# Perceiver on one core: a tile's eight row gathers issued together at its last step

## The reference

```python
x = x + _L0_ffn_ref(_layernorm(x, axis=-1), L0_ffn_gate_w, ...)         # 64 experts, 8 for each token
x = x + _L1_xattn_ref(_layernorm(x, axis=-1), ctx_1024, ctx_1024, ...)  # 8 heads, keys and values of both kinds
# _L0_ffn_ref, its end: each token's eight expert rows are weighed and summed
y = (unsorted.reshape(B * S, TOP_K, D) * topk_w[..., None]).sum(axis=1)
# _L1_xattn_ref: softmax over the scores of both kinds, then values, W_o, layer norm, W_ffn, relu
```

## Time and profile before

| | us |
|---|---|
| median of 3 runs | 3863.2 (3858.03 to 3872.15) |
| the profiled execution | 3865.37 |
| its span, first to last instruction | 3863.6 |
| TensorE matmuls busy | 3139.7 (81%) |
| VectorE busy | 2202.4 (57%) |
| ScalarE busy | 1664.8 (43%) |
| GpSimd busy | 1411.5 (37%) |

### The profile page before, as it was taken

One profiled execution on the slowest core, in us unless ns is written; L12 is line 12 of the kernel. 1 busy time (PEld: TensorE's weight loads), 2 busy tenths in 40 slices (PEclk: granted clock), 3 DMA queues, 4 the chain that ended last, 5 costly groups with the idle time before them and its releaser, 6 DMA issues. The chain is left out here.

```text
span 3863.6 us, 90063 instructions
## 1 busy us (share of the span) xinstructions
PE 3139.7 (81%) x30574; PEld 2540.3 (66%) x30574; DVE 2202.4 (57%) x5866; ACT 1664.8 (43%) x4673; POOL 1411.5 (37%) x2430
## 2 busy tenths in 40 slices
PE   7999999997742006998799999999987777569998
PEld 5666666666642005887677777777765656459998
DVE  4777676766567303665677776667755556641111
ACT  4666666664520002333244444444435556434443
POOL 1222222222237771000777777777632222220000
PEclk9999999998975558999899999999998998769999
DMA  2000000000021413555111111111100000000000
GB/s 78 22 16 22 18 20 22 16 17 2 0 122 50 131 55 112 150 152 146 35 34 33 33 33 33 33 33 33 30 6 2 0 2 0 1 11 12 11 11 22
DMA packets 158242, 150.49 MB, mean 39 GB/s; under 512 B 18680, under 2 KB 137728, under 8 KB 157696
## 3 DMA queue, kind: packets, MB, share of 16 engines
q1 hardware_dynamic: 141696, 114.86, 9.8%
q0 software_dynamic: 16384, 33.59, 2.9%
HBM read 95.95 MB, written 52.43 MB: 38 GB/s over the span
## 5 line engine op out<-in xcount | busy, mean ns | idle before, releaser
L1656 POOL DMA_INDIRECT y_picked<-f_ys,idy x256 | 246.9, 965 | 394.7 <-POOLq L92 352.5
L1523 ACT ACTIVATE y_prob<-y_ps_s,y_mx 128x514 f32<-128x514 f32 x256 | 176.5, 690 | 445.2 <-DVE y_mx L1731 445.2
L2276 POOL DMA_INDIRECT f_xs<-acc,f_idx x256 | 255.8, 999 | 102.3 <-issue 83.3
L1336 PEld LDWEIGHTS y_ps_o<-y_v,y_pT 128*128 128x128 f32 x2048 | 248.8, 191 | 59.7 <-issue 42.0
L1336 PE MATMUL y_ps_o<-y_v,y_pT 128*128 128x64 f32 x2048 | 272.0, 276 | 11.0 <-DVE y_om L1824 9.7
L77 POOL TENSOR_TENSOR x_px<-x_prob,consts 128x64 f32<-128x64 f32 x256 | 75.9, 296 | 560.2 <-ACT x_prob L856 560.2
L2681 ACT ACTIVATE g_hid<-g_ps_h,g_b 128x512 f32<-128x512 f32 x256 | 176.1, 688 | 240.5 <-PE g_ps_h L100 237.8
L856 ACT ACTIVATE x_prob<-x_ps_s,x_mx 128x289 f32<-128x289 f32 x512 | 250.8, 496 | 45.9 <-DVE x_mx L1017 42.3
L2697 DVE SCALAR_TENSOR_TENSOR x<-g_ps_y,g_w_now,x 128x128 f32<-128x128 f32 x256 | 72.1, 344 | 345.5 <-PE g_ps_y L2647 345.5
L1024 DVE COPY x_pT<-x_ps_t 128x512 f32<-128x512 f32 x256 | 177.1, 692 | 144.3 <-PE x_ps_t L644 140.3
L2472 PE MATMUL fe_ps_x<-consts,fe_xg 128*128 128x128 f32 x384 | 75.5, 278 | 208.7 <-DMA fe_xg<-f_xs 208.6
(11 more groups left out here) (443 smaller groups left out, 8779.3 us busy)
## 6 DMA issues: line engine op xcount, KB each, us to landing
fe_xg<-f_xs SPq DMA_DIRECT2D x192, 128.0 KB, 2.1
f_ys<-fe_yk SPq DMA_DIRECT2D x192, 128.0 KB, 2.1
x_ctxT<-ctx_dram SPq DMA_DIRECT2D x32, 514.0 KB, 3.5
y_ctxT<-ctx_dram SPq DMA_DIRECT2D x32, 514.0 KB, 3.6
f_weights<-w_one_dram SPq DMA_DIRECT2D x1, 10240.0 KB, 28.1
f_xs<-f_zeros SPq DMA_DIRECT2D x64, 128.0 KB, 1.8
f_xs<-acc,f_idx POOLq DMA_INDIRECT x256, 2.2
y_picked<-f_ys,idy POOLq DMA_INDIRECT x256, 2.5
```

The lines of the kernel that those rows point to most:

```text
L1336: mm = pe.matmul(ps_o[:, b, at:at + GW], pT[:, u % 2, g, c, :], v[:, b % 2, c, g * D + at:g * D + at + GW], start=(u == 0 and g == 0 and c ...
L1523: ins = act.activation(prob[:, p, :, :], ps_s[:, 2 * p:2 * p + 2, 0:M], ACT.Exp, bias=mx[:, p:p + 1], accum_out=den[:, s, b, p:p + 1])
L1656: pool.indirect_dma_start(out=picked[:, t % 2, k * D:(k + 1) * D], out_offset=None, in_=ys, in_offset=bass.IndirectOffsetOnAxis(ap=idy[:, ...
L2276: pool.indirect_dma_start(out=xs, out_offset=bass.IndirectOffsetOnAxis(ap=idx[:, t, k:k + 1], axis=0), in_=acc[:, t, :], in_offset=None).t ...
```

## The change

The eight gathers of tile t + 3 are no longer issued one at each step of tile t, behind `keep`, but all at step 7, behind `add(t - 1)`. They are the same transfers with the same waits and semaphores; the gathers in `start` are as before.

```diff
                     keep(t, s, u)
                     if u == 1 and nxt:
                         keep_z(t + 1)
-                    if t + 3 < TILES:
-                        pick_row(t + 3, u)
                     if 2 <= u < BT + 2 and nxt:
                         split_ctx(t + 1, n, u - 2)
                     if u == 1 and nxt:
...
                         add_queries(t + 1, n)
                     if u == 7 and prev:
                         add(t - 1)
+                    if u == 7 and t + 3 < TILES:
+                        for k in range(TOP1):
+                            pick_row(t + 3, k)
```

## The result

The changed kernel takes 4328.9 us (median of 4 runs, 4325.9 to 4333.8) against 3865.2 for the kernel before in the same comparison (4 runs): a ratio of 1.120, 95% interval 1.118 to 1.123. The forecast was 4072, with a range up to 4110. The direction, the place and the size of the new wait were right; what lies behind it was taken at a sixth of its size.

The account below looks back on a forecast made before the run. TensorE was taken to bound the stage; 29 bursts x (5.4 stall + 1.8 clock - 0 removed) = 209 us on 3865.4 gave 4074, as a median 4072 us, with a range of 4015 to 4110.

Parts of the forecast that it names:

- What bounds the kernel, and the first wait to come: In cross_attention_two TensorE, 96% busy, sets the pace; with the burst it first misses the keys of scores 2.
- Cover, burst, stall: Ahead of scores 2: 2.9 us to spare, burst from +1.1, ka sum ending at +11.6, new stall 5.4 us a tile.
- rival 3: Steady gathers follow each other at 0.96 us, not 1.26: stall 3.0 us, clock 1.5, 3994 us; chance 0.07.
- What is removed: TensorE's wait for y_ctx_lo goes, but a wait for VectorE's y_ka_sin returns it: 0 us, at most 0.95 a tile.
- What is moved beside: Transfers land with over 9 us to spare before weighing; GpSimd's 1.9 us debt after the stall is paid once.
- The clock of TensorE: Behind each new stall TensorE's clock falls to 1.2 GHz, losing 1.8 us a tile; bounds 0 and 2.9.
- The sum: 29 bursts, 29 x (5.4 + 1.8 - 0) = 209 us more: 4072 us as a median, 5% slower.
- Rival 1: The stall comes, but the clock doesn't fall or its fall is hidden: 4020 us; chance 0.13.
- Rival 4: Half-clock steps behind the stall cost 2.9 us, or the release is 0.33: 4110 us; chance 0.10.
- Rival 2: Burst covered, at 0.55 us a gather or less: 3837 us, chance 0.03, or unchanged at 3863, chance 0.05.

Follow-up runs that it names:

- tuned0: The kernel before, gathers at each step, with VectorE's weighing moved to the end of step 2 and its row sum to step 3: 3832.2 us.
- fill12: The changed kernel with 12 matmuls of constants put where TensorE would wait for y_ka, ahead of scores 2: 4010.6 us.
- fillbehind runs: The changed kernel with 16, 6 or 3 matmuls of constants behind the wait for y_ka, ahead of scores 2: 4287.5, 4163.9 and 4131.8 us.
- fillbehind3: The changed kernel with 3 matmuls of constants behind the wait for y_ka, ahead of scores 2: 4131.8 us.
- last5: The kernel before with the last five gathers of a tile together at step 7, the others at their own steps: 3892.5 us.
- last6: The kernel before with the last six gathers of a tile together at step 7, the others at their own steps: 3986.6 us.
- fill6: The changed kernel with 6 matmuls of constants put where TensorE would wait for y_ka, ahead of scores 2: 4091.5 us.
- step0: The kernel before with all eight gathers of a tile together behind the keep of step 0: 4043.0 us.
- halves04: The kernel before with four gathers behind the keep of step 0 and four behind the keep of step 4: 4003.5 us.
- last7: The kernel before with the last seven gathers of a tile together at step 7, the first at its own step: 4124.2 us.
- tuned3: The kernel before with the last three gathers together at step 7, and VectorE weighing rows at step 1 and summing them at step 3: 3899.4 us.

## Why the prediction was right or wrong

- **What bounds the kernel, and the first wait to come.** Right: TensorE, and the keys of scores 2.
- **Cover, burst, stall.** Right to 0.1 us: start +1.08 (1.1), pitch 1.26 (1.26), end +11.56 (+11.6), wait 5.33 (5.4). The seven pitches in the start of the stage were the row to take, and rival 3 (pitch 0.96) is refuted.
- **What is removed: 0.** Right as a number for this edit: the wait for y_ctx_lo became one for y_ka_sin. Wrong in the general form, that VectorE takes back what GpSimd gives: tuned0 got rid of both waits by moving VectorE's work alone. So the right number came with a reason that was only half of it.
- **What is moved beside.** Right: no wait for the rows, GpSimd's debt is paid by scores 3 (step 3 of fill12 is 4.39 as before).
- **The clock of TensorE.** This is the step that failed. That the clock falls was right, and so was the loss of 0.43 per us of work at the lower level (10.7 measured, 25.0 x 0.43 = 10.8). The term was 4.15 us of work behind each wait, with a bound of 6.8; it measured 25.0. I had carried the length of the low stretch over from other stages, as if it belonged to the wait. The fillbehind runs showed that the work that follows has a large part in it: with three matmuls of 128 x 256 there it is 6.8, without them 27.3 behind the same wait. The trace of before has no steady tile of this stage at the lower level, and my upper bound came from rows of other work. But even that trace had longer stretches than the two that I took, one of 47.8 us up to 1872.1, over the start of this stage, and one of 17.1 us at its end (windows of TensorE in them):

```profile
1840.00:1872.10 32.10, 16.95 (x62) 0.50 0.10 27
2875.70:2892.60 16.90, 6.96 (x26) 0.50 0.00 0
```

They hold many pauses, so they don't give the 25.0 us either, but a bound of 6.8 us had no ground. The bound was too low; a bound for this work was the whole tile at the lower level, 31.7 / 0.57 - 31.7 = 23.9 us, which gives 3865.4 + 29 x (5.4 + 23.9) = 4715 us and holds the time.
- **The sum with the measured term.** 29 x (5.35 + 10.7) = 465, 3865.4 + 465 = 4331; the profiled execution took 4327.4.
- **Rivals.** Rival 1, the stall alone, is what fill12 measures (4010.6 against 4020), and not what the changed kernel did. Rival 4 had the right mechanism, a dearer clock, at a quarter of its size (2.9 for 10.7). Rival 2 is out: the pitch was 1.26, not 0.55. What the Trainium skill, page "TensorE: Matmul & The Clock Gate", section "HAM oscillation — how this bites in real kernels", describes, bursts that run cold behind each wait, held in this trace: the clock fell in each steady tile. Its half of the time lost at the lower level gives an estimated 12.5 a tile for 25.0 us, a little over the measured 10.7.

## What to carry to other kernels

A row of indirect transfers on GpSimd held its queue for 1.25 us each, so put it only where the work queued behind it has that much slack: four (5.0 us) fitted in the 2.9 us of cover, the 1.46 us that GpSimd stood idle ahead of the ka sum, and 0.4 of wait, and the fifth already cost time. When an edit makes a busy TensorE wait in each tile, and the wait is of the length that lowered the clock here (2.7 us in some tiles or in all, 3.5 and more in all), reckon with the work behind the wait at the lower clock, up to the whole tile, not with the length of a fall seen in another stage. Before taking a wait as given back to another engine, look whether both come from one pair of instructions that overlap.

## What the runs showed of the hardware

- TensorE's granted clock stayed at its lower level through 25 us in which TensorE was recorded as busy without a pause, tile after tile, and came back within 6.8 us when three matmuls of 128 x 256 stood first (2.9 us of work, fillbehind3). The Trainium skill, page "TensorE: Matmul & The Clock Gate", section "What's actually happening", ties the level to how busy TensorE has been; by the busy time of the record that doesn't account for the 25 us, and the measurement decides.
- After waits of 1.6 us the clock held but for once in 23 (last5, 1955 to 2700 us); after 2.7 to 2.8 it fell in some tiles and not in others of the same code (last6, fill6), and in step0 in each; after 3.5 (halves04), 4.1 (last7) and 5.3 us (the changed kernel) it fell in each.
- In tuned3 it fell in 4 of some 23 tiles without any wait over 1.0 us for another engine, and in tuned0 once. Why is open.
- A wait of TensorE for GpSimd (0.95 us a tile for `y_ctx_lo`) went when an instruction of VectorE was moved: the ka sum ahead of it on GpSimd took 1.65 us beside that instruction (the kernel before) and 0.74 without it (tuned0).
